# Layer 0's first batch multiplied amid the norm, and the last attention's batches run between its groups' norms

## The reference

```
x = x + L0_attention(ctx, layernorm(x), ctx)     # K, V = ctx @ Wk, Wv;  Q = layernorm(x) @ Wq; 16 heads, causal
...
x = x + L2_ffn(layernorm(x))     # 8 experts, top 2: y = g0 * expert_a(x) + g1 * expert_b(x)
x = x + L3_attention(layernorm(x), ctx, ctx)
#   q = layernorm(x); Q, K, V linear with bias; scores without softmax, so (Q K^T) V = Q (K^T V);
#   o = (Q (K^T V)) Wo + bo;  z = q + o (with the mask's penalty);  result = lng * layernorm(z) + lnb
x = x + L3_ffn(layernorm(x))     # quantized two-layer feed-forward
```

## Time and profile before

| | us |
|---|---|
| median of 3 runs | 1884.29 (1879.65 to 1884.39) |
| profiled execution, its own time | 1887.41 |
| its span | 1885.60 |
| busy in it: PE / DVE / ACT / POOL | 1611.3 / 1069.5 / 892.9 / 374.8 |
| mean granted clock of PE | 0.922 |

### The profile page before, as it was taken

One profiled execution on the slowest core, in us unless ns is written; L12 is line 12 of the kernel. 1 busy time (PEld: TensorE's weight loads), 2 busy tenths in 40 slices (PEclk: granted clock), 3 DMA queues, 4 the chain that ended last, 5 costly groups with the idle time before them and its releaser, 6 DMA issues.

```text
span 1885.6 us, 27943 instructions
## 1 busy us (share of the span) xinstructions
PE 1611.3 (85%) x10002; PEld 1231.2 (65%) x10002; DVE 1069.5 (57%) x3026; ACT 892.9 (47%) x2006; POOL 374.8 (20%) x469
## 2 busy tenths in 40 slices
PE   6999863999769999999858799999998589993666
PEld 5677663888646667767536567767766478893534
DVE  6767741222256766666577665555554434326787
ACT  3888811222136666666549355555553012232266
POOL 1000013111132333333140100000001332223644
PEclk9999966999879999999978899999997699996878
DMA  9000026989500000000000200000000347993001
GB/s 333 2 2 1 2 90 244 297 289 293 185 1 12 7 6 7 7 1 1 1 1 1 79 12 6 6 7 6 1 1 12 137 137 262 307 329 98 0 12 34
DMA packets 61625, 152.26 MB, mean 81 GB/s; under 512 B 8960, under 2 KB 39696, under 8 KB 55248
## 3 DMA queue, kind: packets, MB, share of 16 engines
q1 hardware_dynamic: 54096, 133.91, 21.5%
q0 software_dynamic: 5280, 14.47, 2.0%
q10 hardware_dynamic: 2112, 2.10, 0.4%
HBM read 133.89 MB, written 24.75 MB: 84 GB/s over the span
## 4 chain that ended last, share of the span: by engine, by line
PE 70%; DVE 15%; ACT 5%; issue 4%; POOL 3%; DMA 1%; POOLq 1%; another core or an unknown queue 0%; SPq 0%; DVEq 0%; ACTq 0%
PE bank L931 8%; PE bank L887 8%; PE bank L1325 8%; PE bank L1379 6%; PE bank L1392 6%; PE bank L1366 5%; PE bank L1329 5%; PE bank L1309 3%; PE bank L626 3%; PE bank L1941 2%; PE bank L1728 2%; PE bank L642 2%; PE bank L657 1%; PE bank L282 1%; PE bank L901 1%
## 5 line engine op out<-in xcount | busy, mean ns | idle before, releaser
L1576 DVE TENSOR_REDUCE small<-bank 128x1 f32<-128x512 f32 x128 | 82.5, 686 | 108.7 <-PE bank L1379 108.7
L950 ACT ACTIVATE e2a<-bank,WB 128x128 f32<-128x128 f32 x156 | 44.6, 368 | 188.3 <-PE bank L931 144.3
L1572 DVE CUSTOM_DVE_ANT_0 p1f<-bank,p1f 128x512 f32<-128x512 f32 x128 | 83.2, 687 | 80.9 <-PE bank L1379 80.9
L1450 ACT ACTIVATE p2f<-bank,small 128x512 f32<-128x512 f32 x128 | 86.9, 683 | 86.2 <-DVE small L1576 86.2
L700 ACT ACTIVATE l<-l,small 128x256 f32<-128x256 f32 x256 | 108.9, 502 | 32.5 <-DVE small L767 32.1
L1447 ACT ACTIVATE p1f<-p1f,small 128x512 f32<-128x512 f32 x128 | 91.2, 714 | 67.5 <-DVE small L1572 67.2
L358 POOL TENSOR_SCALAR rs<-mv 128x4 f32<-128x4 f32 x20 | 4.7, 237 | 582.3 <-DVEq L230 551.8
L1325 PE MATMUL bank<-WA,HT 128*128 128x256 f32 x384 | 94.1, 389 | 5.0 <-DVE p1f L1517 5.0
L767 DVE CUSTOM_DVE_ANT_0 l<-bank,small 128x256 f32<-128x256 f32 x256 | 90.8, 421 | 13.2 <-PE bank L642 12.3
L1461 ACT ACTIVATE p2f<-bank 128x512 f32<-128x512 f32 x128 | 75.2, 598 | 40.5 <-PE bank L1366 39.0
L950 ACT ACTIVATE e0a<-bank,WB 128x128 f32<-128x128 f32 x128 | 36.6, 368 | 120.6 <-PE bank L931 120.6
(11 more groups left out here) (385 smaller groups left out, 3951.6 us busy)
## 6 DMA issues: line engine op xcount, KB each, us to landing
WB<-in_L2pack SPq DMA_DIRECT2D x39, 514.0 KB
WB<-in_L2pack SPq DMA_DIRECT2D x39, 512.0 KB
WB<-in_L0pack SPq DMA_DIRECT2D x16, 1028.0 KB
WB<-in_L0pack SPq DMA_DIRECT2D x16, 1024.0 KB
e0a<-in_L0pack SPq DMA_DIRECT2D x7, 1028.0 KB
e0a<-in_L0pack SPq DMA_DIRECT2D x7, 1024.0 KB
sorted_h<-in_blank SPq DMA_DIRECT2D x6, 1032.0 KB, 16.4
e2a<-sorted_h SPq DMA_DIRECT2D x39, 129.0 KB
```

The costliest lines, as they stand in the source:

```text
L1450: ins = a.e.activation(P, k.bank(x), ACT.Exp, bias=self.mx[:, m:m + 1], accum_out=self.sm[:, m:m + 1])
```

## The change

In layer 0, `first` is no longer run behind the norm. The norm's `pe` and `ac` already took a function to be called behind each group; it now runs K of batch 0 on PE behind group 1's transposes, Q behind group 2's and V behind group 3's. DVE copies K behind group 3's rows, ACT copies Q ahead of its copy for group 3. The final copies follow the norm as before.

In layer 3's attention:

- For groups 1 to 3, ACT multiplies part 1 by its gate in place (`second_ac`), POOL adds X to it in one 128x1024 instruction (`second_po`), and DVE's `finish` does one pass (part 0 times its gate, plus that sum) where it did two. Group 0 keeps both passes on DVE.
- Both copies behind the transposes are ACT's (`alone_ac`); DVE has no `turn`.
- PE's order interleaves the groups' transposes (T) with the batches: T0 Q0 Q1 C0, T1 C1 O0 Q2 O1 Q3 C2, T2 C3 O2 Q4 O3 Q5 C4, T3 C5 O4 Q6 O5 Q7 C6, C7 O6 O7. ACT follows this order, with the penalty of a group behind its copies. The transposes keep two banks, the batches take six in turn.
- DVE: finish 0, finish 1, rows 0, finish 2, rows 1, finish 3, rows 2, then the loop; rows of group 3 come at i = 1.
- POOL: add 1, factor 0, add 2, add 3, factor 1, bias 0, factor 2, factor 3, bias 1, then its loop, with the bias of groups 2 and 3 at i = 1 and i = 3. The loop's factors lie in `rs2` instead of `rs`.

```diff
+    def alone_pe(self, t, g):
+        t.wait_ge(self.tok, g + 1)
+        t.wait_ge(self.ha, g)
+        for c in range(2):
+            for j in range(4):
+                ins = t.e.transpose(k.bank(c)[:, j * 128:(j + 1) * 128], self.keep(4 * g + j)[:, c * 128:(c + 1) * 128], k.ident[:, :])
+            ins.then_inc(self.tr.sem, 1)
+    def alone_ac(self, a, g):
+        a.wait_ge(self.tr, 2 * g + 2)
+        for c in range(2):
+            ins = a.e.activation(k.HT[:, c, g * 512:(g + 1) * 512], k.bank(c), ACT.Copy)
+        ins.then_inc(self.ha.sem, 1)
...
+    def early_pe(self, t, g):
+        if g < 3:
+            t.wait_ge(u.cd, (3, 3, 4)[g])
+            t.wait_ge(u.ca, (3, 4, 4)[g])
+            self.pe_piece(t, *self.first[g])
+    def early_dv(self, v, what, g):
+        if (what, g) == ("norm", 3):
+            self.dv_piece(v, *self.first[0])
+    def early_ac(self, a, g):
+        if g == 2:
+            a.wait_ge(self.k.setup.cst, 4)
+            self.ac_piece(a, *self.first[1])
     def pe(self, t):
-        self.norm.pe(t)
+        self.norm.pe(t, lambda g: self.early_pe(t, g))
         self.norm.ready(t, 15)
-        t.wait_ge(k.setup.ca, 4)
-        t.wait_ge(k.setup.cd, 4)
-        for p in self.first:
-            self.pe_piece(t, *p)
...
     def finish(self, v, g):
-        for c in range(topk):
+        summed = topk == 2 and g > 0
+        for c in range(1 if summed else topk):
             v.wait_ge(self.ag[topk * g + c], 1)
+            if summed:
+                v.wait_ge(self.summed, g)
             for t in T:
                 ins = v.e.scalar_tensor_tensor(out=k.X[:, t, :], in0=self.Y[c][:, t, :], scalar=self.gv[:, c, t:t + 1],
-                                               in1=k.X[:, t, :], op0=ALU.mult, op1=ALU.add)
+                                               in1=self.Y[1][:, t, :] if summed else k.X[:, t, :], op0=ALU.mult, op1=ALU.add)
+    def second_ac(self, a, g):
+        a.wait_ge(self.ag[2 * g + 1], 1)
+        for t in range(4 * g, 4 * g + 4):
+            ins = a.e.activation(self.Y[1][:, t, :], self.Y[1][:, t, :], ACT.Copy, scale=self.gv[:, 1, t:t + 1])
+        ins.then_inc(self.worthed.sem, 1)
+    def second_po(self, q, g):
+        y = self.Y[1][:, 4 * g:4 * g + 4, :]
+        q.wait_ge(self.worthed, g)
+        q.e.tensor_tensor(y, y, self.k.X[:, 4 * g:4 * g + 4, :], ALU.add).then_inc(self.summed.sem, 1)
...
+        self.order = [("T", 0), ("Q", 0), ("Q", 1), ("C", 0)]
+        for j in range(1, 4):
+            b = 2 * j
+            self.order += [("T", j), ("C", b - 1), ("O", b - 2), ("Q", b), ("O", b - 1), ("Q", b + 1), ("C", b)]
+        self.order += [("C", 7), ("O", 6), ("O", 7)]
+        self.R = Turns((2, 3, 4, 5, 6, 7), [x for x in self.order if x[0] != "T"])
...
     def po(self, g):
-        self.norm.po(g, lambda j: self.added(g, j))
+        self.layer.second_po(g, 1)
+        self.norm.factor(g, 0)
+        self.layer.second_po(g, 2)
+        self.layer.second_po(g, 3)
+        self.norm.factor(g, 1)
+        self.added(g, 0)
+        self.norm.factor(g, 2)
+        self.norm.factor(g, 3)
+        self.added(g, 1)
         for i in range(9):
...
+            if i in (1, 3):
+                self.added(g, 2 + i // 2)
```

More of the change, by code:

```diff
@@ L305, in dv @@
             elif what == "norm":
[L306 to L315, removed]
+                self.rows_dv(v, g)
             elif what == "turn":
@@ L346, in ac, with po, factor @@
             behind(3)
-    def po(self, g, behind=None):
+    def po(self, g):
+        for j in range(4):
+            self.factor(g, j)
+    def factor(self, g, j):
         k, eps = self.k, 1e-5
[L350 to L362, removed]
+        dst, var = k.rs[:, 4 * j:4 * j + 4], k.mv[:, 4 * j:4 * j + 4, 1]
+        g.wait_ge(self.stat, j + 1)
+        if self.twice:
+            g.chain(g.e.tensor_scalar(dst, var, 1.0 + eps, eps * eps, ALU.mult, ALU.add))
+        else:
+            g.chain(g.e.tensor_scalar(dst, var, eps, None, ALU.add))
+        g.e.tensor_tensor(dst, dst, k.nhalf[:, 0:4], ALU.pow).then_inc(self.rsd.sem, 1)
     def ready(self, seat, t):
         seat.wait_ge(self.ha, t // 4 + 1)
-        seat.wait_ge(self.hd, t // 4 + 1)
+        if self.hd is not None:
+            seat.wait_ge(self.hd, t // 4 + 1)
 class Setup:
@@ L685, in ac @@
         k = self.k
[L686 to L689, removed]
+        self.norm.ac(a, lambda g: self.early_ac(a, g))
+        self.ac_piece(a, *self.first[2])
         for n, (mid, end) in enumerate(self.steps):
@@ L1999, in pe @@
         self.fence.pass_(t, "pe")
-        self.norm.pe(t)
         t.wait_ge(*self.ready_w)
[L2002 to L2009, removed]
+        for what, b in self.order:
+            if what == "T":
+                self.norm.alone_pe(t, b)
+                continue
+            bk = k.bank(self.R.bank((what, b)))
+            self.free(t, (what, b))
+            if what == "Q":
+                lo = b * 256
+                self.norm.ready(t, 2 * b)
                 for c in range(2):
@@ L2038, in ac @@
         self.fence.pass_(a, "ac")
[L2039 to L2044, removed]
+        for j in range(1, 4):
+            self.layer.second_ac(a, j)
+        for what, b in self.order:
+            if what == "T":
+                self.norm.alone_ac(a, b)
+                self.penalty(a, b)
+            elif what == "Q":
+                bk = k.bank(self.R.bank(("Q", b)))
+                a.wait_ge(self.qm, b + 1)
+                a.wait_ge(self.cm, b - 2)
                 for c in range(2):
-                    ins = a.e.activation(self.Qs[i % 3][:, c, :], bk[:, c * 256:(c + 1) * 256], ACT.Identity, bias=k.col("bq", c))
+                    ins = a.e.activation(self.Qs[b % 3][:, c, :], bk[:, c * 256:(c + 1) * 256], ACT.Identity, bias=k.col("bq", c))
                 ins.then_inc(self.qb.sem, 1)
-            b = i - 1
-            if 0 <= b < 8:
+            elif what == "C":
                 a.wait_ge(self.cm, b + 1)
@@ L2057, in dv @@
         self.fence.pass_(v, "dv")
-        self.norm.dv(v)
+        for j in range(4):
+            self.layer.finish(v, j)
+            if j:
+                self.norm.rows_dv(v, j - 1)
         for i in range(10):
+            if i == 1:
+                self.norm.rows_dv(v, 3)
             if i == 7:
```

57 lines of the change are left out of this document (30 added, 27 removed).

## The result

The kernel after took 1870.83 us (median of 7 runs, 1866.31 to 1874.68), the kernel before 1884.39 (7 runs, 1879.65 to 1888.60): ratio 0.9924, 95% interval [0.9909, 0.9939], 13.6 us less by the medians and 14.3 by the ratio. Forecast were 7.0 less, 1877.3. The direction was right and the median lies inside the range of 1870.5 to 1884, just above its lower end, but the change is twice the one forecast. The profiled execution of after has a span of 1865.7 us, 19.9 less than before's; the medians differ by 13.6, so part of that difference belongs to the two executions and not to the change.

A forecast was written before the change was run, and what follows sets the result against it. Program order was taken to bound the start, DVE and POOL the end of layer 3's attention. Gains of 4.2 us in layer 0 and 2.8 in attention, 7.0 together, gave 1877.3 us, range 1870.5 to 1884.

The forecast's parts named there:

- Layer 0: Start: K, Q and V of batch 0 run between the norm's transposes, scores at 27.8 instead of 32.2; 4.2 us gained.
- Rival A: Layer 0: clock falls anyway or weights come late; 1 to 2.6 us gained there, 1880 in all; chance 0.12.
- Attention up to the first output: Layer 3's attention: despite new waits, PE's batches start earlier and the first output comes 9.7 us ahead.
- DVE's wait for POOL's first sum: Layer 3's attention, group 1: DVE waits 2.9 us for POOL's add, and everything behind it on DVE waits too.
- Group 0's rows held up beside POOL's sums: Layer 3's attention: these DVE rows meet POOL's adds for groups 2 and 3, done at 1725.6 instead of 1721.4.
- Rival D: Layer 3's attention: PE's short bursts never raise the clock; slower, 1898 us with layer 0's gain; chance 0.07.
- The failed step: Layer 3's attention, behind the first output: POOL's pace and bias adds cut the 9.7 us lead to 2.8.
- its own sign of being wrong: Layer 3's attention: the prediction counts as wrong if the lead at the end exceeds 5 us.
- Rival B: Layer 3's attention: POOL eats the whole lead; 4.2 us gained in all, 1880; chance 0.14.
- rival C: Layer 3's attention: the lead survives, 7.3 us plus layer 0's 4.2, giving 1872.8; chance 0.07.
- the replay: Layer 3's attention: in-order queues replayed with profiled durations; end lead 1.9 us against the trace, 3.3 against the old order's replay.
- side sentence: Layer 3's attention: by the skill's rule the last gated DVE pass waits some 2 us for a bias add, end 0.2 later.

The follow-up runs named there:

- order only: The change, but DVE does both scaled passes of every group, without ACT's scaling and POOL's sums; ratios to the kernel before 0.9921 and 0.9916.
- e2: Not a run: a stage with experts in the untouched middle; from its last gate matmuls to its first expert, 77.0 and 66.0 us with the same kernel on two chips.

## Why the prediction was wrong in size

**Layer 0: right.** K was forecast at 19.2 and ran at 19.18, Q at 23.2 (22.63), V at 26.0 (25.23), scores at 27.8 (27.0 to 27.7 in all runs with this part), clock 1.00. The term was 4.2; the marks of profiles with and without this part, on one chip, give 4.4 to 5.2. They hold 0.4 in after that came before the moved work, where group 1's transposes ran at 17.5 instead of 17.9. Rival A is out.

**Attention up to the first output: right, step by step.** DVE's wait for POOL's first sum: 2.9 forecast, 3.16 measured. Group 0's rows held up beside POOL's sums: done at 1725.6 forecast, 1711.15 + 14.05 = 1725.2 measured. The clock rose 3.2 us after unbroken work began by forecast; it was low to 1718 on after's axis, 3.6 behind 1714.4. The first output was to come 9.7 ahead and came 9.9 ahead. Rival D, in which the clock stays low, is out: 0.94 in the three us behind 1718.

**The failed step** is the one behind the first output, in the prediction's words: "From here POOL, with its 4.16 a batch and DVE's rows stalling beside it, sets the pace; the bias add of group 3 (2.34) also comes inside." Of the 9.7 it let 2.8 survive; the term measured 5.6 (6.0 to 6.3 beside the old attention on the same chip), over the 5 that the prediction had named as its own sign of being wrong. So the step failed by its prices for DVE's and POOL's meetings and for the adds: it charged 6.9 behind the first output, where 4.3 were lost. Rival B (the whole lead is eaten) and rival C (all but one add survives, 7.3) are both out. The loss in detail, on before's axis, with DVE's additions to X: batch 0 at 1753.1 where it was 1759.3, 6.2 ahead (its shift ended 5.1 ahead, 3.8 by forecast); batch 2 at 1763.0 (1768.0), 5.0 ahead; the feed-forward's early rows at 1773.9 (1779.2), 5.3 ahead, where 1777.0 was forecast. So 3.7 are lost up to batch 0, 1.3 between batches 1 and 2, where group 3's bias add lies (5.62 between two additions instead of 4.3), and behind it nothing. The add is not the cause of most of that: without it the two additions are still 5.26 apart. Elsewhere the first four batches keep the 4.3 that they had in before. By the prediction's own words the replay priced the meetings too high, its old order ending 1.4 late. Against the trace it gave 1.9 at the end, and 2.8 were taken; the truth was 5.6.

Two things in that step were wrong beside its size. Bias adds that are moved behind batch 0's shift give back no more than 0.3, so the order of POOL's queue was not what held the end. And POOL's adds are only half of what is lost: without them 2.2 of the 4.3 remain. What the timelines show there is PE's third output 9.5 behind the first instead of 8.6, with transposes between them, and DVE's rows of group 3 (1.94) between the first two; that these make up all of the 2.2 was not tried, and it stays open.

**What the split was worth** the prediction did not ask, since it replayed both edits as one. It costs 3.3 to 3.7 us in this order, and 3.8 to 4.5 together with ACT's copies in the old one. The sentence on the three sums was there (DVE waits, the rows are held), and its price against 5.1 us of DVE passes taken away was never set beside it. Without the split the attention's lead is over 9.

**The rest of the 13.6** is not in the prediction's terms. The marks of the change sum to about 11; the two later comparisons hold that. That the measured time fell inside the range, and near rival C's 1872.8, is luck: C's lead of 7.3 did not occur, and 2 to 3 of the 6.5 us between forecast and result are in neither of the change's stages.

**The best version** is order only: ratios 0.9921 and 0.9916, against 0.9924, 0.9933 and 0.9944 of the change. The intervals overlap, so what is shown is the stage (76.7 and 76.9 against 80.2 to 80.4), and what is likely is that it is 3 us faster as a whole.

## What to carry to other kernels

When two edits serve one aim, price each without the other: here one brought all of the gain and the other cost a third of it. Before work is taken from DVE and given to POOL, set the DVE time saved against the wait for POOL's result and against the DVE instructions held up beside it: here 1.7 a group against 3.16 and 2.23 at the first. When a replay of the old order ends late against the trace, suspect its prices for collisions; with more collisions in the new order the correction may have to be larger than the lateness, as here. And set marks on the engine whose work was moved: PE's first output gave stretches that repeat within 0.1, DVE's mark did not separate the two edits.

## What the hardware did that I had not expected

- **Who waits when DVE and POOL meet.** DVE's four scaled rows take 1.35 alone and took 3.58 when POOL's sum was already running (1707.57). DVE's gated pass at 1715.77, begun 0.24 ahead of POOL's bias add, took its usual 1.67, and the add took 3.64 instead of 2.34: here POOL waited. As the prediction applied the Trainium skill's rule in its side sentence, this pass would have waited some 2 us. The Trainium skill (SBUF — State Buffer, "Who interferes with whom") says that "Issue order, not op shape, decides who blocks"; both rows agree with it.
- **Not every collision lengthens the stage.** DVE's normalizing of two tiles takes 0.70 beside two small instructions of POOL (128x2) and 1.01 to 2.39 beside its larger ones in after, 0.80 us for one tile in the mean; nevertheless the additions to X of batches 0 and 1, and of 2 and 3, are 4.3 apart as in before. That the engine held up had the time to spare is my reading; no run isolates it.
- **The same kernel differs by 11 us in one stretch from chip to chip** (order only, 77.0 and 66.0 around `e2`'s sorting). A span of one execution can't be set against another's for a change of this size; stretches cut at marks inside the touched stages repeat within 0.7, and those from PE's first output within 0.1.
